# A two-layer graph-attention kernel: the next group's first-layer statistics and normalisation moved to a later place in each pass

## The reference

```python
h = jnp.maximum(_layernorm(x, axis=-1), 0.0)
x = x + _L0_gnn_ref(h, adj, ...)      # layer 0
h = jnp.maximum(_layernorm(x, axis=-1), 0.0)
x = x + _L1_gnn_ref(h, ..., adj)      # layer 1
```

```python
# layer 0: 12 heads of 32
h = jnp.einsum('bnd,ade->bane', feat_in, W)
th = jnp.tanh(h)
attn = th @ w_src + swap(th @ w_dst); attn = leaky_relu(attn, 0.2)
attn = softmax(where(mask, -999.0, attn))
feat_out = elu(attn @ h + b)
gate = sigmoid(feat_in @ H_w.T + H_b)
return gate * feat_out + (1.0 - gate) * feat_in
# layer 1: 6 heads of 64
q, k, v = x @ Wq + bq, x @ Wk + bk, x @ Wv + bv
probs = softmax(q @ k.T / 8 + where(adj, 0, -9e15))
return (probs @ v) @ Wf + bf
```

## Time and profile before

| | |
|---|---|
| median of 3 runs | 1215.11 us (1213.73 to 1215.54) |
| the profiled execution's own time | 1212.82 us |
| its span, first to last instruction | 1211.0 us |
| mean granted TensorE clock | 0.933 of full |
| PE busy | 1034.0 us (85%) |
| PE weight loads busy | 894.5 us (74%) |
| DVE busy | 770.3 us (64%) |
| ACT busy | 588.1 us (49%) |
| POOL busy | 258.8 us (21%) |

### The profile page before, as it was taken

One profiled execution on the slowest core, in us unless ns is written; L12 is line 12 of the kernel. 1 busy time (PEld: TensorE's weight loads), 2 busy tenths in 40 slices (PEclk: granted clock), 3 DMA queues, 4 the chain that ended last, 5 costly groups with the idle time before them and its releaser, 6 DMA issues.

```text
span 1211.0 us, 24852 instructions
## 1 busy us (share of the span) xinstructions
PE 1034.0 (85%) x10153; PEld 894.5 (74%) x10153; DVE 770.3 (64%) x1456; ACT 588.1 (49%) x1126; POOL 258.8 (21%) x338
## 2 busy tenths in 40 slices
PE   4779888897988879888898888979888799889876
PEld 4577868777786777868777686768867778688765
DVE  6567658476583757757476583866847476585734
ACT  5646274461735626364361744626455262745421
POOL 2140131402213031130401313022130401313020
PEclk9779999899898999999899898999989899999988
DMA  8211121411113132121311213122231311213102
GB/s 211 28 27 27 53 29 28 79 28 54 27 28 80 28 72 26 38 52 28 80 28 54 27 28 80 28 62 24 49 54 28 80 28 55 27 29 53 28 26 53
DMA packets 183653, 56.41 MB, mean 47 GB/s; under 512 B 164979, under 2 KB 183541, under 8 KB 183541
## 3 DMA queue, kind: packets, MB, share of 16 engines
q1 hardware_dynamic: 183540, 54.83, 23.4%
HBM read 17.06 MB, written 12.58 MB: 24 GB/s over the span
## 4 chain that ended last, share of the span: by engine, by line
PE 52%; DVE 26%; DMA 9%; issue 6%; ACT 5%; SPq 1%; POOL 0%; DVEq 0%; ACTq 0%; POOLq 0%
PE ps L611 10%; PE ps L597 10%; PE ps L613 10%; PE ps L612 10%; DMA x_in<-in_x_dram 5%; DVE stats L823 4%; PE ps L775 4%; PE ps L679 4%; DMA out_dram<-x_in 4%; DVE x L923 3%; DVE p L948 3%; DVE ee L920 3%; DVE mx L946 3%; DVE p L901 3%; ACT p L420 2%
## 5 line engine op out<-in xcount | busy, mean ns | idle before, releaser
L400 POOL TENSOR_TENSOR x_in<-x_in,ee 128x384 f32<-128x384 f32 x64 | 69.3, 1083 | 695.9 <-DVE ee L926 695.9
L459 ACT ACTIVATE th<-ps 128x384 f32<-128x384 f32 x64 | 31.3, 489 | 307.7 <-DVE v_tok L911 307.7
L597 PE MATMUL ps<-ident,p 128*128 128x128 f32 x576 | 96.1, 330 | 47.3 <-DVE p L901 36.9
L823 DVE BATCH_NORM_STATS2 stats<-x_in 128x6 f32<-128x384 f32 x128 | 63.2, 547 | 107.1 <-DMA x_in<-in_x_dram 107.1
L597 PEld LDWEIGHTS ps<-ident,p 128*128 128x128 f32 x576 | 83.7, 172 | 52.1 <-DVE p L901 39.1
L597 PE MATMUL ps<-ident,th 128*128 128x128 f32 x192 | 48.5, 391 | 78.5 <-ACT th L459 78.5
L959 DVE COPY_PREDICATED_SCALAR z<-not_adj,masked 128x768 f32 x64 | 69.3, 1083 | 66.3 <-ACT z L491 66.3
L988 DVE TENSOR_TENSOR hT1l<-ps,hT1h 128x512 fp32r<-128x512 f32 x48 | 31.7, 689 | 110.0 <-ACT hT1h L530 109.1
L597 PEld LDWEIGHTS ps<-ident,th 128*128 128x128 f32 x192 | 34.1, 197 | 89.6 <-ACT th L459 89.5
L497 ACT ACTIVATE z<-z 128x768 f32<-128x768 f32 x64 | 54.6, 853 | 62.0 <-DVE z L964 60.5
L611 PE MATMUL ps<-Wf_hi,hT1h 128*128 128x384 f32 x192 | 70.7, 368 | 5.5 <-DVE hT1l L1024 5.3
(11 more groups left out here) (129 smaller groups left out, 2860.8 us busy)
## 6 DMA issues: line engine op xcount, KB each, us to landing
V<-v_tok SPq DMA_DIRECT2D x128, 192.0 KB, 4.7
x_in<-in_x_dram SPq DMA_DIRECT2D x16, 768.0 KB, 4.6
out_dram<-x_in SPq DMA_DIRECT2D x16, 768.0 KB, 3.6
x<-in_L_gnn_H_w_dram SPq DMA_DIRECT2D x1, 576.0 KB, 5.9
QT<-in_L_gnn_W_dram SPq DMA_DIRECT2D x3, 192.0 KB, 6.7
thT<-in_L_gnn_Wq_dram SPq DMA_DIRECT2D x1, 576.0 KB, 6.1
z<-in_L_gnn_Wk_dram SPq DMA_DIRECT2D x1, 576.0 KB, 7.2
z<-in_L_gnn_Wv_dram SPq DMA_DIRECT2D x1, 576.0 KB, 8.2
```

The lines of the kernel that those rows point to most:

```text
L400: pool.tensor_tensor(x_in[:, i % 3, t], x_in[:, i % 3, t], ee[:, t], ALU.subtract).then_inc(x2_made, 1)
L597: return pe.transpose(dst, src, ident[0:rows, 0:rows])
L823: dve.bn_stats(stats[:, layer, t], src).then_inc((stats0, stats1)[layer], 1)
```

## The change

Three pieces of work for the next group keep their instructions but stand elsewhere in their engine's list. On DVE `norm0(i + 1)` stood behind `values0(0)`, and now stands behind the expansion of the block-diagonal rows. On ACT `normalise0(i + 1)` stood behind the two copies of the logit rows, and now stands behind the first exponential, `exp0(0)`. On POOL `inv_std(0, i + 1)` stood directly behind `inv_std(1, j)`, and now stands behind the additions of the bias and of `h0` into `x_in`. SP's and PE's lists keep their order.

```diff
@@ POOL
                 if real(j):
                     inv_std(1, j)
-                if real(i + 1):
-                    inv_std(0, i + 1)
                 if real(j):
                     pool.wait_ge(h1_made, TILES * (j + 1))
@@
                         pool.tensor_tensor(x_in[:, i % 3, t], x_in[:, i % 3, t], h0[:, par, t], ALU.add).then_inc(x_plus_h, 1)
+                if real(i + 1):
+                    inv_std(0, i + 1)
+                if real(i):
                     pool.wait_ge(x_plus_h, TILES * (i + 1))
@@ ACT
-                if real(i + 1):
-                    normalise0(i + 1, 1 - par)
                 copy_q(0)
@@
                 exp0(0)
+                if real(i + 1):
+                    normalise0(i + 1, 1 - par)
@@ DVE
                 values0(0)
-                if real(i + 1):
-                    norm0(i + 1)
                 values0(1)
@@
                         .then_inc(dst_blocks_made, 1)
+                if real(i + 1):
+                    norm0(i + 1)
                 softmax0(0)
```

## The result

The changed kernel takes 1103.61 us (median of 4 runs, 1103.48 to 1106.03) against 1215.25 us for the kernel before. The ratio is 0.9088, with a 95% interval of 0.9073 to 0.9104. The forecast was 1102.0 us.

The account below looks back on a forecast made before the run. It took DVE's statistics waiting for the load behind each store as the bound: 13 periods of 64.47 us against 73.08 save 111.9 us; with −1.7 and +0.5, 1099.7, plus 2.3 to the median: 1102 us, range 1095 to 1125.

Parts of the forecast that it names:

- The stretch from the store to the masks: First part of each of 13 periods: evacuations wait only for PE, as in pass 15; 34.33 us, taken from there.
- The stretch from the masks to the store: Rest of each of 13 periods: taken unchanged from one period of the kernel before, 30.14 us.
- DVE's and ACT's new places: Statistics behind the expansion, normalise0 behind exp0(0): cost nothing; without the gap 2.3 us, without the cover 2.5 us a pass.
- POOL: inv_std(0, i + 1) behind the additions: cost nothing, the shift 2.0 us after the statistics.
- Passes 0 and 1: Pass 1: ACT's wait for the second evacuation goes, −1.7 us; pass 0: transposes of h0 may wait for normalise0, +0.5 us.
- The last two periods: End of the kernel: the forecast's sum has no term for a change there.
- The sum: Whole kernel: 1212.82 − 111.9 − 1.7 + 0.5 = 1099.7 us, plus 2.3 to the median, so 1102 us.
- this rival: Transposes at the start of a pass: PE's clock falls there, 1.7 us a pass, 22 us in all, 1124 us; chance 0.16.
- the last rival: DVE's new place: late load stalls softmax0(0), costing from 16.7 us after the store; no change 0.02, slower (1220 us) 0.02.

Follow-up runs that it names:

- The kernel without the late loads: The kernel before, its order kept, with the 13 loads of x behind a store left out (output not the reference's): 1107.17 us, ratio 0.9118.
- the second trace: The changed kernel itself, unaltered, timed again with another trace: 1105.11 us, ratio 0.9099 to the kernel before.
- The filling: The changed kernel plus 10 unread products per pass on PE, in its wait behind the last attention product: 1095.94 us, 0.9029; with 14 products 1098.14 us, 0.9043.
- The load behind the block-diagonal rows: The changed kernel with the load of x issued only when the block-diagonal rows are expanded, about 14.8 us after the store: 1103.71 us, ratio 0.9087.

## Why the prediction was right

**The stretch from the store to the masks** (the main term). Taken from pass 15 as 34.33 us. In the 13 periods after, it is 34.29 to 34.66 us, 34.40 on average. Right to 0.1 us. The kernel without the late loads shows that the cause was the load, as the prediction said.

**The stretch from the masks to the store.** Taken as 30.14 us, from one period. It is 29.97 to 30.79 us after the change, 30.53 on average, and 30.46 in the second trace. This is the term that was mis-sized, by 0.3 to 0.4 us a pass, 4 to 5 us in all. Before, the 13 periods average 30.17, so the one I took was fair. The sum took the clock behind the last wait as unchanged. It was 1.00 in 5 of 13 periods of before, and is in 1 of 13 in one trace of the changed kernel and in 5 of 13 in the other, so the number of such passes doesn't explain the difference by itself. The passes in which it falls have become dearer: their stretch was 29.99 to 30.58 us before and is 30.35 to 30.92 now. The filling shows that the clock is what costs, for with it the stretch is 29.97 in most passes. Why a fall costs more now than before stays open.

**DVE's and ACT's new places.** Costs of nothing, as predicted, with 2.15 us left ahead of the softmax (forecast 2) and 2.7 us ahead of the masks (forecast 2.4).

**POOL.** The shift comes 2 us behind the statistics. The prediction gave this move no price, and the kernel without it confirms that.

**Passes 0 and 1.** Forecast −1.2 us together, measured −2.44 at the first store, and −1.53 in the second trace (142.60). Pass 0 costs 0.7 us (its last DVE statistics begin at 77.78 instead of 77.04). There PE does wait for `normalise0`, as the prediction feared:

```profile
52.64 3.87 PE L598 MATMUL ps<-ident,h 128*128 128x128 f32 x12 [3.17 <-ACT h L413]
```

Pass 1 gains 3.2 us and not 1.7. The forecast took only ACT's wait; the granted clock around the transposes there was 0.54 before and is 1.00 in this trace. It is 0.82 over the same 7 us in the second, so part of this gain comes and goes.

**The last two periods** are 1.6 us longer in the first trace (114.49 against 112.90) and unchanged in the second (112.86), as the prediction had them.

**The sum, and what was luck.** The first trace gives −2.4 − 105.9 + 1.6 = −106.8 us for the span, the second −1.5 − 108.0 − 0.0 = −109.6 us (span 1101.4). The forecast had −113.1, so it was 3.5 to 6.3 us too good by the traces. By the medians it was 1.5 us too good (−111.6), and 3.6 by those of the second timing (−109.6). The mechanism and the main term were right. That the median came out only 1.6 us from the forecast is in part luck: the second timing of the same kernel lies 3.1 us from it.

**The rivals.** The clock did not fall in the 24 transposes (1.00). The rule of the Trainium skill behind this rival, from "TensorE: Matmul & The Clock Gate", section "Part 4: PE-mode transpose", speaks, taken by itself, for a fall. The trace does not agree: 24 transposes behind dense products run at a clock of 1.00 in all 13 periods. But the clock did fall in another place that the prediction's rivals had not named. The threshold in the last rival was too strict. I had put it at a landing 16.7 us after the store, where the room ahead of the softmax ends. The load behind the block-diagonal rows lets the statistics begin 614.33 − 595.09 = 19.2 us after it, at no cost, since DVE has further idle time behind the first softmax tiles.

## What to carry to other kernels

If one pass of a pipeline lacks the step in question (here the last, without a next group), it shows in advance what the others will look like without it; a stretch of it is worth more than a sum of instruction times. Put a wait for a transfer where the engine has idle time behind it and where what queues behind it isn't asked for soon; what counts is the room behind it and not the wait's length alone: 4.57 us cost nothing here, 8.95 us cost 3.6 us a pass. Move the steps that depend on it along with it: with DVE's step moved alone, ACT took over the wait and gave most of the gain back.

## What the runs showed of the hardware that I had not expected

A wait of PE of only 2.3 us, behind short matmuls of 64 rows, is followed by 3 us at a granted clock between 0.50 and 0.58 (nearly all at the lower level, 1.2 GHz) in 12 of 13 passes and 1.00 in the thirteenth, at the same place with the same work. In another execution of the same kernel it is 8 passes (0.50 to 0.52) against 5. Ten products of no use in the wait keep the clock at 1.00 behind it in all 13 and save 9 us of 1105. What PE did around the wait (transposes and short matmuls ahead of it, transposes behind it) may count too; which part of it does was not tested.
